# Attention with a layer norm and a quantised feed-forward block on one core: which queries a maxima step takes as its tile

## The reference

```python
x = x + attention(layernorm(x))        # 16 heads of 64, 2048 x 2048 scores for each head
x = x + ffn(layernorm(x))              # gate, up, silu, down; inputs and weights quantised to FP4 in blocks of 16

# attention, for each head
sim  = einsum('id,jd->ij', q, k) / sqrt(64)
attn = softmax(sim, axis=-1)           # subtracts the row's maximum before the exponential
out  = einsum('ij,jd->id', attn, v)    # then out @ w_out + b_out
```

## Time and profile before

| | |
|---|---|
| median of 3 runs | 1382.57 us (1380.14 to 1383.19) |
| the profiled execution: time | 1384.4 us |
| the profiled execution: span, first to last instruction | 1381.5 us |
| TensorE busy (matmuls) | 1299.0 us, 94% of the span |
| TensorE weight loads busy | 674.4 us, 49% |
| GpSimd busy | 1053.9 us, 76% |
| ScalarE busy | 897.7 us, 65% |
| VectorE busy | 798.2 us, 58% |
| mean granted TensorE clock | 0.978 of full speed |

### The profile page before, as it was taken

The page is one execution under the profiler, slowest core; times in us unless marked ns, Lnnn a source line. Parts: engine busy times, 40 slices in busy tenths (PEclk is TensorE's granted clock), DMA queues, the critical chain, the costliest instruction groups (busy, mean ns, idle before and its releaser), DMA issues.

```text
span 1381.5 us, 24376 instructions
## 1 busy us (share of the span) xinstructions
PE 1299.0 (94%) x7541; PEld 674.4 (49%) x7541; DVE 798.2 (58%) x2142; ACT 897.7 (65%) x1300; POOL 1053.9 (76%) x457
## 2 busy tenths in 40 slices
PE   4999999999999999999999999999999999898466
PEld 3555555555455555555445555555555454343245
DVE  6655555555455555555555555555555556777694
ACT  4767666677666766677666676667767667554242
POOL 4488878898778878888788888888988888789232
PEclk9999999999999999999999999999999999999787
DMA  2000000000000000000000000000000000000001
GB/s 61 2 9 2 1 2 9 2 1 1 3 9 2 2 1 9 2 1 1 3 9 2 2 1 9 2 2 1 3 1 1 1 2 1 2 1 1 1 1 30
DMA packets 18300, 6.63 MB, mean 5 GB/s; under 512 B 9696, under 2 KB 18016, under 8 KB 18160
## 3 DMA queue, kind: packets, MB, share of 16 engines
q1 hardware_dynamic: 17936, 4.40, 1.4%
q0 software_dynamic: 224, 0.54, 0.1%
HBM read 3.75 MB, written 1.05 MB: 3 GB/s over the span
## 4 chain that ended last, share of the span: by engine, by line
PE 85%; DVE 7%; issue 4%; POOL 2%; ACT 0%; DMA 0%; POOLq 0%; SPq 0%; DVEq 0%; ACTq 0%
PE o_ps L1151 32%; PE s_ps L1000 24%; PE mx_ps L1023 7%; PE mx_ps L1016 5%; PE misc_ps L1141 3%; PE s_ps L1008 2%; PE misc_ps L1133 2%; PE misc_ps L971 2%; PE misc_ps L983 1%; PE misc_ps L972 1%; PE misc_ps L973 1%; POOL acc_pool L497 1%; PE misc_ps L984 1%; PE misc_ps L985 1%; PE s_ps L1243 1%
## 5 line engine op out<-in xcount | busy, mean ns | idle before, releaser
L497 POOL TENSOR_TENSOR acc_pool<-acc_pool,probs 128x1024 f32<-128x1024 f32 x352 | 853.4, 2424 | 49.5 <-POOL acc_pool L497 40.3
L614 ACT ACTIVATE probs<-s_ps 128x1024 f32<-128x1024 f32 x512 | 527.3, 1030 | 122.1 <-PE s_ps L1008 67.3
L790 DVE CUSTOM_DVE_ANT_0 summed<-mx_ps,rise 128x512 bf16<-128x512 f32 x503 | 344.8, 686 | 424.9 <-issue 354.5
L1151 PE MATMUL o_ps<-probs,vv 128*64 128x512 f32 x2048 | 498.5, 607 | 5.1 <-ACT probs L614 5.1
L534 ACT ACTIVATE rise<-mx_ps 128x512 f32<-128x512 f32 x503 | 301.2, 599 | 271.7 <-PE mx_ps L1016 261.1
L1151 PEld LDWEIGHTS o_ps<-probs,vv 128*64 128x64 f32 x2048 | 127.2, 136 | 229.5 <-issue 174.8
L1016 PE MATMUL mx_ps<-k_raw,q_hi 64*128 64x512 f32 x503 | 224.5, 446 | 10.5 <-DVE part_max L790 9.2
L1023 PE MATMUL mx_ps<-k_hi,q_hi 64*128 64x512 f32 x503 | 224.5, 446 | 1.9 <-DVE part_max L790 1.8
L1000 PE MATMUL s_ps<-q_hi,k_hi 64*128 64x512 f32 x1024 | 207.0, 399 | 0.9 <-ACT probs L614 0.8
L1000 PE MATMUL s_ps<-q_hi,k_lo 64*128 64x512 f32 x1024 | 202.6, 390 | 0.0
L1000 PE MATMUL s_ps<-q_lo,k_hi 64*128 64x512 f32 x1024 | 202.4, 390 | 0.0
(11 more groups left out here) (161 smaller groups left out, 1119.0 us busy)
## 6 DMA issues: line engine op xcount, KB each, us to landing
wqkv<-in_L_attn_w_qkv SPq DMA_DIRECT2D x8, 192.0 KB, 3.3
y<-in_L_attn_x SPq DMA_DIRECT2D x4, 256.0 KB, 4.6
mrow<-neg_max SPq DMA_DIRECT2D x64, 2.0 KB, 2.0
out<-y SPq DMA_DIRECT2D x4, 256.0 KB, 2.3
wo<-in_L_attn_w_out SPq DMA_DIRECT2D x8, 64.0 KB, 1.9
wx<-in_L_ffn_w_down POOLq DMA_DIRECT2D x1, 176.0 KB, 6.6
wx<-in_L_ffn_w_gate POOLq DMA_DIRECT2D x1, 128.0 KB, 4.3
wx<-in_L_ffn_w_up POOLq DMA_DIRECT2D x1, 128.0 KB, 4.9
```

The lines of the kernel that those rows point to most:

```text
L497: pool.tensor_tensor(acc, first, probs[:, j % P_BUFS, :, :], ALU.add) \
L614: act.activation(probs[:, j % P_BUFS, :, :], s_ps[:, j % 2, :, :], ACT.Exp, scale=SCALE) \
L790: dve.tensor_tensor_reduce(summed[:, s % 2, :], mx_bank(h, pair), rise[:, h, :], 1.0, LOWEST, ALU.add, ALU.max, part_max[:, slot:slot + 1] ...
L1151: ins = pe.matmul(o_ps[DH * h:DH * (h + 1), :], vv[par(w)][:, j, DH * h:DH * (h + 1)], probs[:, j % P_BUFS, h, :], start=(j == 0), stop=(j ...
```

## The change

A maxima step takes every fourth query of the chunk as its tile: tile `t` is the queries `4*p + t` for p = 0 to 127. So place `4*p + t` of `mrow`, which the transfer writes as before, now holds the maximum of query `4*p + t`: the row lies in order of the queries, and `maximum` reads it as it lies. The weight loads of `base` and `step_up` now read `q_hi` with a step of four numbers, 16 bytes, where they read 128 numbers in a row. Nothing else differs: the same instructions are issued in the same order on every engine, with the same waits.

```diff
                 for h in range(2):
                     rows = slice(DH * h, DH * (h + 1))
-                    ins = pe.matmul(s_ps[:, buf, h, :].rearrange("p (t q) -> p t q", t=TQ), ones_r[rows, :],
-                                    mrow[rows, :].rearrange("p (q t) -> p t q", t=TQ), start=False, stop=True,
+                    ins = pe.matmul(s_ps[:, buf, h, :], ones_r[rows, :], mrow[rows, :], start=False, stop=True,
                                     skip_group_check=True)
                 return ins
 
+            def query_tile(q, rows, t):
+
+                return q_hi[q][rows, :].rearrange("p (q t) -> p t q", t=TQ)[:, t, :]
+
             def base(h, i, k, q, pair):
 
                 rows, (g, t) = slice(DH * h, DH * (h + 1)), divmod(i, TQ)
-                return pe.matmul(mx_bank(h, pair), q_hi[q][rows, t * P:(t + 1) * P], k_raw[k][rows, g * QC:(g + 1) * QC],
+                return pe.matmul(mx_bank(h, pair), query_tile(q, rows, t), k_raw[k][rows, g * QC:(g + 1) * QC],
                                  start=True, stop=True)
 
             def step_up(h, i, k, q, pair):
 
                 rows, (g, t) = slice(DH * h, DH * (h + 1)), divmod(i, TQ)
                 moving = k_hi[k][rows, :].rearrange("p (c f n) -> p c f n", f=2, n=HALF)[:, 2 * g:2 * g + 2, 1, :]
-                return pe.matmul(mx_bank(h, pair).rearrange("p (c n) -> p c n", n=HALF), q_hi[q][rows, t * P:(t + 1) * P],
+                return pe.matmul(mx_bank(h, pair).rearrange("p (c n) -> p c n", n=HALF), query_tile(q, rows, t),
                                  moving, start=True, stop=True)
```

## The result

The changed kernel takes 1415.16 us (median of 4 runs, 1411.38 to 1416.26) against 1382.76 us before: 2.4% slower, ratio 1.0237 with a 95% interval of 1.0224 to 1.0249. Its profiled execution has a span of 1412.5 us, 31.0 us more than before. The forecast was 1376.4 us, and the range ended at 1391 us.

What follows compares the result with a forecast made beforehand. TensorE was taken to bound the kernel (85% of the chain). The row's gain of 6.2 us, with nothing for stepped loads, took the median from 1382.57 to 1376.4 us; range 1373 to 1391 us.

Steps and rivals of the forecast that it cites:

- The gain from the row: `maximum` at each unit's start: contiguous reading saves 0.20 us in 30 units plus 0.2 us once, 6.2 us.
- the second call's saving: `maximum` for key tile 1: 0.21 us saved becomes waiting for tile 0's exponential; rival that it is kept, chance 0.04.
- The price of a stepped load: Uncovered weight loads of maxima steps, 239 on the chain: bounded from nothing to a factor of two, taken as nothing.
- the first rival: Uncovered loads behind `weighted` and `rise` pay: factor of two, 26.3 us, chance 0.12; addition per column, 12.5 us, chance 0.10.
- the price of nothing: Weight loads of maxima steps: stepped loads already keep 0.86 ns per column and lose nothing; forecast's chance 0.62.
- the two others: Uncovered weight loads: addition for each column, 1388.9 us, chance 0.10; factor of two, 1402.7 us, chance 0.12.
- The places: Uncovered maxima pairs behind `weighted` and `rise`: eight for each of 31 units, 239 counted on the chain.
- the extra 15 us of the rival's upper end: Odd maxima steps: if load latency counts, 0.06 us over cover in 248 pairs, taking the factor of two to 1418 us.
- (1): Sign at `maximum`: mean duration near 450 ns instead of 661, and 0.23 us from second call to next possible pair.
- (4): Sign in the unit's period: it shrinks by 0.20 us, with the same shift on all engines.
- (2): Sign at maxima-step weight loads: they stay at 184 ns, and in even steps the next load comes 0.11 us behind.
- (3): Sign at a unit's start: the wait of L1000's weight loads for the exponential grows from 0.46 to about 0.66 us.

Runs made afterwards that it cites:

- the row alone: Kernel before with `maximum` reading the row contiguously and weight loads unchanged, so queries get maxima of other queries of their chunk: 1377.48 us against 1381.48 us.
- a longer start on ScalarE: Kernel before plus a second copy of q, sorted by tiles, written by ScalarE, from which the maxima steps load; row read contiguously: 1379.91 us, ratio 0.9997.
- a step of two: Changed kernel with tiles of every second query of half a chunk, loads stepping 8 bytes, row read as pairs of neighbours: 1384.67 us, ratio 1.0024.
- eight transfers: Kernel before with eight transfers of 128 x 1 numbers per unit instead of two, ordering the row, which is read contiguously: 1380.06 us, ratio 0.9989.
- four transfers: Tiles of every second query of half a chunk, row ordered by four transfers of 128 x 2 numbers and read contiguously: 1380.3 us against 1381.58.

## Why the prediction was wrong

*The gain from the row* was right in its steps. `maximum` costs 0.23 us, its mean is 456 ns (forecast near 450), the unit's start moved forward by 0.20 us, and the second call's saving turned into a wait of 0.21 us. With the row alone the period fell by 0.21 us. The total is 4.0 us where 6.2 were expected; the shortfall lies in single places and not in the usual units.

*The price of a stepped load* is the step that failed: "I take nothing, because the two numbers of 0.86 ns agree so closely". The measured price is 0.13 us for each uncovered pair. It was the first rival, the factor of two, whose price of 0.11 us was a little low. The reason given for nothing was that both read paths were held to the same pace. They are not. The load is as fast at 8 bytes as contiguous, within 8 ns, and slower at 12 and 16. The moving operand is as slow at 8 bytes, and in pairs of neighbours, as at 16. It is not any gap that slows it: the moving operand of `step_up` is two runs of 256 columns with a gap between them, and its pair is followed by the next after 0.25 us (584.50 to 584.75), as the timeline of the kernel before shows:

```profile
584.75 0.40 PE L1000 MATMUL s_ps<-q_hi,k_hi 64*128 64x512 f32 x2
```

Runs between 2 and 256 columns were not measured. The trace before had no stepped load, so it could not tell this; the equality of two numbers from two paths was no evidence for a common rule. The upper bound of 0.11 us was nearly right, but the price of nothing was given a chance of 0.62 against 0.22 for the two others, and the range stopped at 1391.

The rule that the Trainium skill gives (Advanced Engine Details and Errata, section Memory Cachelines) is nearer: two hits on a line of 16 bytes are needed. For loads the runs agree: full pace at 8 bytes, 192 against 184 ns, and a penalty at 12 and 16. For the moving operand they don't: at 8 bytes, with two hits, it takes the same 0.53 us as at 16, and pairs of neighbours, with two hits as well, take 655 ns against 456. Here the measurement decides.

*The places* were counted rightly: eight in a unit, and 8 x 0.13 - 0.21 = 0.83 us, against 0.81 in the usual unit. Odd steps were covered even at 0.30 us, so the extra 15 us of the rival's upper end did not come; only in every fourth unit did one of them lose its cover, at 0.3 us. One count was read wrongly: of the 503 loads in a group 11 belong to the prologue and not to the steady part (of 512 steps the prologue makes 20, 9 of them into other banks).

*The prologue* was missing from the sum. I had counted only the eight places of the steady units. In the prologue the pairs stand between short projections and their loads are uncovered too: a pair and its projection took 0.91 us and take 1.03 at full clock. And with stepped loads the granted clock fell to half from 37.5 to 58 us. Together that cost 9.1 us by unit 1. Without the prologue the first rival's sum with the measured price is 1382.6 - 6.2 + 239 x 0.13 = 1407.5 us, and the run with contiguous loads in the prologue measured 1407.93. That they agree so closely is partly luck: the row gave 4.0 us and not 6.2, the fourth units lose more, and that run's kernel before had 1381.24 us. As differences it is 24.9 us against 26.7.

*My checks:* (1) and (4) in its sign were met for the row alone; (2) failed, as the text said would decide. (3) was badly put: the loads' idle time stayed at 0.48 us, since the second call's own load moved forward with the rest. What grew is the gap behind the second call's matmuls, 0.21 us.

## What to carry to other kernels

Before moving a step from one operand to another, count how often each is read and which of the reads nothing covers: here 64 pairs of matmuls were mended at the price of about 500 pairs of loads, half of them uncovered. An access that no row of the trace shows deserves a range as wide as its bounds, and the cheap way out of it is one run with several steps in one kernel. Count the prologue too: here a delay of 0.12 us for each maxima pair, between projections of 128 columns, went with a fall to half the granted clock and 9 to 10 us.

## What the runs showed of the hardware

- A weight load of 128 columns of four bytes takes 184, 192, about 250 and 306 ns with steps of 4, 8, 12 and 16 bytes; from 8 bytes on this is 1.8 ns for each 16 bytes touched. It costs nothing beside 0.23 us of matmuls, and 0.13 us for a pair at 16 bytes where nothing covers it.
- A moving operand of 512 columns: 0.23 us for a pair when contiguous; 0.44 at a step of 16 bytes and for pairs of neighbours 16 bytes apart. At 8 bytes it was read in the first call alone, at 0.53 us, as at 16 (0.34 when contiguous).
- The granted clock fell to half for about 20 us in the prologue with stepped loads (0.12 us longer for each pair), and in one profile with a longer start on ScalarE and contiguous loads. It fell for 3 to 10 us at the start of the first unit in four profiles without steps of 16 bytes in the loads: the row alone, a step of two, eight transfers and four transfers. It was full again in the first unit in all of them, at 49.6 us at the earliest and 58.5 at the latest. What tips it in a single execution is open.
